# A gated graph layer on one core: the sums of the second layer start at -h, and the end stage takes their difference to h as it stands

## The chip, the cores and the metric

One Trainium2 chip, of which the kernel uses one core. The metric is the device time of one execution in microseconds, the median of several runs. The engines are named PE (TensorE, matrix products), DVE (VectorE), ACT (ScalarE), POOL (GpSimd) and SP (SyncE, which here only issues DMAs).

## What is computed

6250 nodes with 128 features, 200,000 edges sorted by their destination. Two graph layers follow one another. The change concerns the end of the second one. Cut to what matters (all in float32):

```
x1   = layernorm(x + layer0(x, edges))                 # first layer
h    = relu(layernorm(x1 @ W1 + b1) * g1 + bt1)
w    = sigmoid(relu([h[src], h[dst]] @ We1 + be1) @ We2 + be2)     # one weight per edge
aggr = segment_sum(w * h[src], dst)
gate = sigmoid([h, aggr] @ Wg + bg)                    # Wg: 256 x 128, its halves Wg_h and Wg_a
new  = gate * aggr + (1 - gate) * h
out  = layernorm(x1 + layernorm(new) * g2 + bt2)
```

## The kernel before

The nodes are 49 blocks of 128, taken in 13 groups of 4 (the last group has 1). Tensors named "cols" have features in the partitions and nodes in the columns: `sums[:, 0, :]`, called `aggr`, holds the sums of either layer that way, and `h_cols` holds h. Five stages follow one another:

1. Edges of layer 0 (to 402 us): sums of the edge features by destination, in `aggr`.
2. Middle stage (402 to 557 us), 13 groups through a pipeline over all engines: `mean_mm` (PE) reads a group of `aggr`; from it come x1, then h, then two tables in device memory, `src_table` and `dst_table`. The groups are interleaved by `run_stages` (L1969): at step t each engine does, in the order of its list, function f for group t - d, where d is the number beside f. On DVE the list is norm1 (4), pre (1), soft_sum (2), moments1 (3), norm2 (6), moments2 (5), rest (11), part2 (12), blank (3). On POOL it is residual (2) and gain (6); gain is two operations, L871 and L873. On ACT, h_turned (8) writes `h_cols` of a group. DVE's blank (L1763) sets the group's columns of `aggr` to zero, once mean_mm has read them, so that the sums of layer 1 can be added there.
3. Edge loop of layer 1 (557 to 2104 us): POOL gathers rows of `src_table` with one indirect DMA per 128 edges (L894), and DVE adds each result to its columns of `aggr` (L546).
4. End stage (from 2105.7 us), 13 groups: PE makes the gate's argument from `h_cols` and `aggr` (gate_mm, L1433 and L1434, two products of 512 columns each, of two PE instructions each), ACT the sigmoid (gate, L1175, into `pre`), POOL the difference aggr - h (apart, L914, into `soft`) and its product with the gate (mix_mul, L921, into `y1`), DVE adds h (mix, L1937, into `aggr`), PE transposes (mix_turn, L1287), ACT copies to `x_rows` (mix_out, L1180), and DVE takes mean and variance (moments3: L1722, L1725). `pre`, `soft` and `y1` have two buffers each, so mix_mul of group g waits for mix of group g - 2, and gate of group g for mix_mul of group g - 2. On DVE the order is mix (g), moments3 (g - 2); on PE gate_mm (g), mix_turn (g - 3); on POOL apart (g), mix_mul (g - 1).
5. Output stage (from 2149.7 us): normalization, g2, bt2, addition of x1, second normalization (L1734, four blocks a group), output. POOL has two operations a group there (L930, L934).

Waits: `need(eng, "name", g)` lets an engine wait until the step "name" has been done for group g. An engine takes its instructions in order.

The functions that the diff touches:

Of the kernel before, what the change touches and what calls it, by code (L numbers as in the profile page):

```python
# [17 lines left out]
ALU = mybir.AluOpType  # L18
# [5 lines left out]
P = 128  # L24
# [17 lines left out]
def gnn_pair(nc, n_nodes, n_edges, io):  # L42
# [13 lines left out]
    n_classes = len(CLASSES)  # L56
    tokens = SORTED * J
    class_cells = [n_blocks * cap for _, _, cap in CLASSES]
    class_cell0 = [sum(class_cells[:k]) for k in range(n_classes)]
    cells = sum(class_cells)  # L60
# [12 lines left out]
    for k, (_, _, cap) in enumerate(CLASSES):  # L73
        per = COLS // cap
        for b in range(0, n_blocks, per):
            riders_of.append((k, range(b, min(b + per, n_blocks))))
    n_riders = len(riders_of)
    GB = 4
    n_groups = -(-n_blocks // GB)
    blocks_of = [min(GB, n_blocks - GB * g) for g in range(n_groups)]  # L80
# [8 lines left out]
    with ctx:  # L89
        def sb(name, shape, dt=F32):  # L90
            return ctx.enter_context(nc.sbuf_tensor(name, shape, dt))

        def sem(name):
            return ctx.enter_context(nc.semaphore(name))
# [8 lines left out]
        aggr = sums[:, 0, :]  # L103
# [4 lines left out]
        h_cols = sb("h_cols", [P, padded])  # L108
# [56 lines left out]
        wg_h = sb("wg_h", [P, P])  # L165
        wg_a = sb("wg_a", [P, P])
# [37 lines left out]
        def temp(cols, dt=F32, depth=2):  # L204
            a = ring[:, at[0]:at[0] + cols * depth]
            at[0] += cols * depth
            a = a if dt == F32 else a.bitcast(dt)
            return a.rearrange("p (s c) -> p s c", s=depth)

        GC = GB * P  # L210
        pre = temp(GC)
        soft = temp(GC)
        y1 = temp(GC)
# [103 lines left out]
        place_dst = yard(2 * RIDE).rearrange("p (s k n) -> p s k n", s=2, k=COLS)  # L317
        cell_logit = yard(4 * COLS).rearrange("p (s k) -> p s k", s=4)
        U_SLOTS, BLOCKS = 3, COLS // min(cap for _, _, cap in CLASSES)
        src_part = spare_ring(U_SLOTS * BLOCKS * P).rearrange("p (s b f) -> p s b f", s=U_SLOTS, b=BLOCKS)  # L320
        h_part = spare_ring(U_SLOTS * BLOCKS * P).rearrange("p (s b f) -> p s b f", s=U_SLOTS, b=BLOCKS)
# [98 lines left out]
        def done(name):  # L420
            if name not in names:
                names[name] = sem("s_" + name)
            return names[name]

        def need(eng, name, n):

            if n >= 0:
                eng.wait_ge(done(name), n + 1)

        def loaded(eng, name, n=1):  # L430

            eng.wait_ge(done(name), 16 * n)
# [12 lines left out]
        def block_cols(g):  # L445
            return slice(g * GC, g * GC + blocks_of[g] * P)
# [339 lines left out]
        def _(eng):  # L786
# [80 lines left out]
            def gain(g):  # L867
# [4 lines left out]
                need(eng, "gain", g)  # L872
                eng.tensor_tensor(z, z, wide["bt1"][:, :].unsqueeze(1).to_broadcast([P, nb, P]), ALU.add).then_inc(done("offset"), 1)  # L873

            loaded(eng, "small", N_SMALL)
            loaded(eng, "x_rows", 2 if tail_nodes else 1)
            run_stages(n_groups, [(2, residual), (NORM2_AT, gain)])


            eng.wait_ge(done("mean_mm"), n_groups)  # L880
# [27 lines left out]

            eng.wait_ge(done("acc2_all"), 1)

            def apart(g):
                cols = block_cols(g)
                need(eng, "mix_mul", g - 2)
                eng.tensor_tensor(soft[:, g % 2, 0:blocks_of[g] * P], aggr[:, cols], h_cols[:, cols], ALU.subtract).then_inc(done("apart"), 1)  # L914

            def mix_mul(g):
                n = blocks_of[g] * P
                need(eng, "apart", g)
                need(eng, "gate", g)
                need(eng, "mix", g - 2)  # L920
                eng.tensor_tensor(y1[:, g % 2, 0:n], soft[:, g % 2, 0:n], pre[:, g % 2, 0:n], ALU.mult).then_inc(done("mix_mul"), 1)  # L921

            run_stages(n_groups, [(1, mix_mul), (0, apart)])


            for g in range(n_groups):
# [518 lines left out]
        def _(eng):  # L1445
# [16 lines left out]
            for g in range(row_groups):  # L1462
                n = min(P, n_chunks - g * P)
# [5 lines left out]
            for g in range(row_groups):  # L1469
                n = min(P, n_chunks - g * P)  # L1470
# [289 lines left out]
                need(eng, "part2", g - 2)  # L1760
                eng.tensor_tensor(r, bank[5][:, 0:nb * P].rearrange("p (b f) -> p b f", b=nb), three[:, :, 0, :], ALU.subtract).then_inc(done("rest"), 1)

            def blank(g):  # L1763
                need(eng, "mean_mm", g)
                eng.memset(aggr[:, block_cols(g)], 0.0)

            def part2(g):
                nb = blocks_of[g]
                three = dst_out[:, g % 2, 0:nb * PARTS * P].rearrange("p (b s f) -> p b s f", s=PARTS, f=P)
                r = rest[:, g % 2, 0:nb * P].rearrange("p (b f) -> p b f", b=nb)  # L1770
                need(eng, "part1", g)
                eng.tensor_tensor(three[:, :, 2, :], r, three[:, :, 1, :], ALU.subtract).then_inc(done("part2"), 1)

            run_stages(n_groups, [
                (4, norm1), (1, pre_), (2, soft_sum), (3, moments1_), (NORM2_AT, norm2), (5, moments2_),
                (DST_AT + 1, rest_), (DST_AT + 2, part2), (3, blank)])
            eng.drain()
            if columns > padded:
                step(eng.memset(aggr[:, padded:columns], 0.0))

# [183 lines left out]
NORM2_AT = 6  # L1964
DST_AT = 10
# [3 lines left out]
def run_stages(n, stages):  # L1969

    for t in range(n + max(d for d, _ in stages)):
        for d, f in stages:
            if 0 <= t - d < n:
                f(t - d)
# [34 lines left out]
```

## Time and profile before

| | us |
|---|---|
| median of 3 runs | 2201.44 |
| lowest and highest | 2198.95 and 2205.48 |
| the profiled execution | 2202.91 |
| its span | 2201.2 |
| middle stage | 402 to 557 |
| edge loop | 557 to 2104 |
| end stage up to the last mean and variance | 2105.7 to 2148.7 |
| output stage | 2149.7 to 2201.2 |

The span is what the profiler saw from the first instruction to the last; the execution's own time has 1.7 us more. Times of single instructions are given from the start of the span. In a timeline one row is one instruction, or several in a row of the same line and shape (x4), with their time together; a bracket behind it is the idle time of the engine before it and what ended that. The time of an instruction is from its issue to its end and includes what it waits for inside.

### The profile page before, as it was taken

To read this page: it belongs to the slowest core of one execution; us is meant where nothing else is said; L and a number is where in the kernel's file an instruction comes from. 1 tells how busy PE (TensorE), PEld (TensorE's weight loads), DVE (VectorE), ACT (ScalarE), POOL (GpSimd) and SP (SyncE) were. 2 spreads that over 40 slices of the span, in tenths; PEclk is the share of its full clock that TensorE was granted. 3 is DMA by queue.
4 is the path that set the end of the run, shared out by engine and by line. 5 is a ranking of instruction groups with operands and counts; after the bars stand their busy time and mean duration, and the time that the engine had idled before them with its cause. 6 is when DMAs were issued, how large, how long until landed. Compare 5 with 4: busy or idle time off the path is not lost.

```text
span 2201.2 us, 43991 instructions
## 1 busy us (share of the span) xinstructions
PE 1621.5 (74%) x13238; PEld 1452.1 (66%) x13239; DVE 1705.9 (77%) x7202; ACT 1070.7 (49%) x2826; POOL 1437.0 (65%) x1437
## 2 busy tenths in 40 slices
PE   4999996898477467777877877767667767877780
PEld 3777775776366467777777876766666667777640
DVE  7777886595899578887888887888876776777666
ACT  0111111375776046665666665766654544555325
POOL 4354430152777777777777777777777777777765
PEclk9999998687555557766767677898788786767675
DMA  7788898014544546556556566666666566666402
GB/s 275 261 298 286 289 336 286 27 47 157 176 127 138 159 127 177 169 170 181 172 166 181 158 181 189 179 189 181 176 198 195 173 193 192 188 188 186 131 1 59
DMA packets 279081, 394.16 MB, mean 179 GB/s; under 512 B 75155, under 2 KB 178612, under 8 KB 278715
## 3 DMA queue, kind: packets, MB, share of 16 engines
q1 hardware_dynamic: 217155, 226.47, 32.4%
q0 software_dynamic: 57408, 156.84, 24.5%
q10 hardware_dynamic: 4280, 8.03, 1.1%
q8 instruction: 107, 1.75, 0.3%
q14 instruction: 131, 1.07, 0.1%
HBM read 376.07 MB, written 15.12 MB: 178 GB/s over the span
## 4 chain that ended last, share of the span: by engine, by line
POOL 46%; PE 24%; issue 19%; DVE 7%; DMA 2%; DVEq 1%; ACTq 1%; ACT 1%; SPq 0%; POOLq 0%
POOL x_rows L894 34%; POOL ring L894 11%; PE bank L495 9%; PE bank L502 3%; PE bank L1289 3%; PE bank L542 2%; DVE bank L531 1%; PE bank L1261 1%; DMA x_rows<-src_table,lane_src 1%; DVE sums L1813 1%; PE bank L1233 1%; DMA ring<-src_table,lane_src 1%; DVE stats L1722 1%; PE bank L1298 1%; ACTq L974 1%
## 5 line engine op out<-in xcount | busy, mean ns | idle before, releaser
L894 POOL DMA_INDIRECT x_rows<-src_table,lane_src x900 | 888.9, 988 | 298.9 <-issue 271.8
L531 DVE SCALAR_TENSOR_TENSOR bank<-bank,we_all 128x128 f32<-128x128 f32 x1686 | 431.6, 324 | 11.1
L894 POOL DMA_INDIRECT ring<-src_table,lane_src x296 | 286.0, 966 | 90.2 <-issue 89.3
L546 DVE TENSOR_TENSOR sums<-sums,bank 128x128 f32 (+1 forms) x814 | 206.2, 253 | 150.1 <-issue 89.3
L1369 PE MATMUL bank<-ring,sums 128*128 128x128 f32 x980 | 274.1, 369 | 46.6 <-DVE bank L531 46.1
L527 DVE TENSOR_TENSOR bank<-bank,x_rows 128x512 f32<-128x512 f32 x225 | 146.4, 696 | 194.5 <-DMA x_rows<-src_table,lane_src 194.4
L1100 ACT ACTIVATE ring<-sums,be_all 128x4 f32<-128x4 f32 (+1 forms) x124 | 36.9, 297 | 508.8 <-DVE bank L531 508.8
L542 PEld LDWEIGHTS bank<-weighted,x_rows 128*128 128x128 f32 x1800 | 280.2, 245 | 0.0
L542 PE MATMUL bank<-weighted,x_rows 128*128 128x40 f32 x1800 | 279.0, 325 | 0.0
L522 PE MATMUL bank<-ring,onehot_t 120*128 120x128 bf16 x1196 | 135.7, 282 | 161.8 <-issue 84.6
L495 PE MATMUL bank<-ring 128*64 128x128 f32 x3128 | 221.8, 285 | 30.4 <-issue 25.3
L531 DVE DVE_READ_ACCUMULATOR bank<-bank,we_all 128x1 f32 x1686 | 235.7, 140 | 0.1
L1347 PE MATMUL bank<-sums 128*128 128x98 bf16 (+1 forms) x736 | 93.5, 299 | 187.9 <-issue 131.7
L1369 PEld LDWEIGHTS bank<-ring,sums 128*128 128x128 f32 x980 | 191.3, 242 | 53.1 <-DVE bank L531 53.0
L522 PEld LDWEIGHTS bank<-ring,onehot_t 120*128 120x128 bf16 x1196 | 109.9, 131 | 169.1 <-issue 168.3
L495 PEld LDWEIGHTS bank<-ring 128*64 128x64 f32 x3128 | 174.2, 140 | 55.0 <-issue 37.7
L1347 PEld LDWEIGHTS bank<-sums 128*128 128x128 bf16 x736 | 74.0, 131 | 203.2 <-issue 199.4
L995 ACT ACTIVATE ring<-bank 128x128 f32<-128x128 f32 x196 | 54.2, 277 | 298.7 <-PE bank L502 282.8
L1371 PE MATMUL bank<-ring,sums 128*128 128x128 bf16 x1470 | 197.3, 254 | 0.0
L1392 PE MATMUL bank<-sums 128*128 128x128 f32 x980 | 188.2, 356 | 0.0
L1392 PEld LDWEIGHTS bank<-sums 128*128 128x128 f32 x980 | 180.5, 275 | 0.0
L1134 ACT ACTIVATE sums<-sums,ones 128x512 f32<-128x512 f32 (+1 forms) x248 | 164.1, 709 | 8.8 <-issue 0.3
(250 smaller groups left out, 3386.2 us busy)
## 6 DMA issues: line engine op xcount, KB each, us to landing
ring<-in_edge_attr SPq DMA_DIRECT2D x195, 512.0 KB, 5.0
ring<-rel_table SPq DMA_DIRECT2D x74, 512.0 KB
ring<-cell_table SPq DMA_DIRECT2D x121, 256.0 KB
ring<-src_table SPq DMA_DIRECT2D x144, 128.0 KB
x_rows<-src_table,lane_src POOLq DMA_INDIRECT x900
ring<-dst_table SPq DMA_DIRECT2D x299, 32.0 KB
ring<-src_table SPq DMA_DIRECT2D x104, 64.0 KB
src_table<-ring SPq DMA_DIRECT2D x12, 512.0 KB, 3.7
```

The source lines that it names most:

```text
L495: last = eng.matmul(out, hot[:, j, :], v[:, j, :], start=(j == 0), stop=(j == J - 1), skip_group_check=True)
L522: last = eng.matmul(out[:, j, :], hot_t[:, j, :], win, start=True, stop=True, skip_group_check=True)
L527: return eng.tensor_tensor(out, out, rows_[:, :, 0:P], ALU.add)
L531: last = eng.scalar_tensor_tensor(hid[:, j, :], hid[:, j, :], 0.0, wide["we2"][:, :], ALU.max, ALU.mult, accum_out=out[:, j:j + 1])
L542: last = eng.matmul(out, rows_[:, j, P:2 * P], hot[:, j, :], start=(j == 0), stop=(j == J - 1))
L546: return eng.tensor_tensor(table[..., bass.ds(start, width)], table[..., bass.ds(start, width)], part, ALU.add)
L894: eng.indirect_dma_start(gathered(c)[:, j, :], None, src_table, bass.IndirectOffsetOnAxis(ap=lane_src[:, t:t + 1], axis=0)).then_inc(gathe ...
L1134: last = eng.activation(hot_, hot_, ACT.Relu, bias=ones[:, 0:1], scale=-1.0)
L1347: eng.matmul(cell_sums(k, v), rows_[:, i, v, :], cols_[:, i, :], start=(t == first and v == 0), stop=(t == end - 1), skip_group_check=True)
L1369: eng.matmul(o, src_hot[:, u % 2, e], src_part[:, u % U_SLOTS, col_block(u, i), :], start=True, stop=False, skip_group_check=True)
L1371: last = eng.matmul(o, dst_hot[:, u % 2, e], base_dst[:, k % 2, s, :], start=False, stop=(s == PARTS - 1), skip_group_check=True)
L1392: eng.matmul(weight_out(q, col_block(u, i)), place_src[:, u % 2, i, :], place_dst[:, u % 2, i, :], start=(i % cap == 0), stop=(i % cap == ...
```

## The change

POOL writes -h into a group's columns of `aggr` in the middle stage, in a new function less_h, in place of DVE's blank, which goes. The sums of layer 1 are then added to -h, so that `aggr` holds (sum - h) at the end. The end stage has no apart; mix_mul reads `aggr` directly. As the argument of the gate is now made from h and (sum - h), the weights of h become Wg_h + Wg_a, which POOL adds once. less_h waits for mean_mm and h_turned of its group and has the offset 9 in POOL's list. DVE waits for all of less_h in place of a drain before it clears the last columns of `aggr`.

```diff
@@ POOL, middle stage
+            def less_h(g):
+                need(eng, "mean_mm", g)
+                need(eng, "h_cols", g)
+                eng.tensor_scalar(aggr[:, block_cols(g)], h_cols[:, block_cols(g)], -1.0, None, ALU.mult).then_inc(done("less_h"), 1)
+
             loaded(eng, "small", N_SMALL)
             loaded(eng, "x_rows", 2 if tail_nodes else 1)
-            run_stages(n_groups, [(2, residual), (NORM2_AT, gain)])
+            eng.tensor_tensor(wg_h[:, :], wg_h[:, :], wg_a[:, :], ALU.add)
+            run_stages(n_groups, [(2, residual), (NORM2_AT, gain), (NORM2_AT + 3, less_h)])
@@ POOL, end stage
-            def apart(g):
-                cols = block_cols(g)
-                need(eng, "mix_mul", g - 2)
-                eng.tensor_tensor(soft[:, g % 2, 0:blocks_of[g] * P], aggr[:, cols], h_cols[:, cols], ALU.subtract).then_inc(done("apart"), 1)
-
             def mix_mul(g):
                 n = blocks_of[g] * P
-                need(eng, "apart", g)
                 need(eng, "gate", g)
                 need(eng, "mix", g - 2)
-                eng.tensor_tensor(y1[:, g % 2, 0:n], soft[:, g % 2, 0:n], pre[:, g % 2, 0:n], ALU.mult).then_inc(done("mix_mul"), 1)
-
-            run_stages(n_groups, [(1, mix_mul), (0, apart)])
+                eng.tensor_tensor(y1[:, g % 2, 0:n], aggr[:, block_cols(g)], pre[:, g % 2, 0:n], ALU.mult).then_inc(done("mix_mul"), 1)
+
+            for g in range(n_groups):
+                mix_mul(g)
@@ DVE, middle stage
-            def blank(g):
-                need(eng, "mean_mm", g)
-                eng.memset(aggr[:, block_cols(g)], 0.0)
-
@@
-                (DST_AT + 1, rest_), (DST_AT + 2, part2), (3, blank)])
-            eng.drain()
+                (DST_AT + 1, rest_), (DST_AT + 2, part2)])
+            eng.wait_ge(done("less_h"), n_groups)
             if columns > padded:
                 step(eng.memset(aggr[:, padded:columns], 0.0))
```

## Rows read from the trace of the kernel before

**Rows 1.** The page: busy time, share of the span and instructions of each engine

```profile
PE 1621.5 (74%) x13238; PEld 1452.1 (66%) x13239; DVE 1705.9 (77%) x7202; ACT 1070.7 (49%) x2826; POOL 1437.0 (65%) x1437
```

**Rows 2.** Timeline of POOL, end stage: start, duration, engine, line, operation

```profile
2123.15 1.27 POOL L914 TENSOR_TENSOR ring<-sums,h_cols 128x512 f32<-128x512 f32 x1
2124.50 1.60 POOL L921 TENSOR_TENSOR ring<-ring 128x512 f32<-128x512 f32 x1
...
2143.45 0.45 POOL L914 TENSOR_TENSOR ring<-sums,h_cols 128x128 f32<-128x128 f32 x1
```

**Rows 3.** Timeline of DVE, end stage

```profile
2121.99 0.86 DVE L1722 BATCH_NORM_STATS2 stats<-x_rows 128x6 f32<-128x128 f32 x4
2122.92 0.38 DVE L1725 BATCH_NORM_AGGREGATE ring<-stats 128x2 f32<-128x6 f32 x4
2123.23 1.74 DVE L1937 TENSOR_TENSOR sums<-ring,h_cols 128x512 f32<-128x512 f32 x1
...
2143.52 0.93 DVE L1937 TENSOR_TENSOR sums<-ring,h_cols 128x512 f32<-128x512 f32 x1
...
2148.56 0.18 DVE L1725 BATCH_NORM_AGGREGATE ring<-stats 128x2 f32<-128x6 f32 x1
```

**Rows 4.** Timeline of PE, end stage: the first two transposes

```profile
2115.32 0.60 PE L1287 MATMUL bank<-ident,sums 128*128 128x128 f32 x4
...
2117.48 0.60 PE L1287 MATMUL bank<-ident,sums 128*128 128x128 f32 x4
```

**Rows 5.** Timeline of ACT, end stage: the gate

```profile
2117.68 0.69 ACT L1175 ACTIVATE ring<-bank,bg_col 128x512 f32<-128x512 f32 x1 [0.98 <-PE bank L1434]
```

**Rows 6.** Windows: length, busy PE, PEld, DVE, ACT, POOL, granted clock, DMA

```profile
2105.70:2111.50 5.80, 5.80 (x8) 2.46 (x9) 0.00 (x0) 0.69 (x1) 2.44 (x2) 0.53 0.01 1
...
2123.20:2134.80 11.60, 9.49 (x34) 4.27 (x33) 11.31 (x38) 4.69 (x8) 11.29 (x9) 1.00 0.00 0
```

**Rows 7.** By line: duration ns min/median/max, first and last start, shape

```profile
L1765 DVE MEMSET sums<- x13: 165/485/485, 420.7 to 511.8; 128x512 f32 x12, 128x128 f32 x1
L819 POOL TENSOR_SCALAR x_rows<-x_rows x25: 1137/1152/1576, 43.6 to 282.4; 128x372 bf16<-128x372 f32 x25
```

**Rows 8.** Timeline of POOL, one step of the middle stage

```profile
448.07 1.26 POOL L871 TENSOR_TENSOR ring<-ring,g_all 128x512 f32<-128x512 f32 x1 [1.22 <-DVE ring L1734]
449.41 1.27 POOL L873 TENSOR_TENSOR ring<-ring,bt_all 128x512 f32<-128x512 f32 x1
453.15 1.27 POOL L865 TENSOR_TENSOR ring<-ring,x_rows 128x512 f32<-128x512 f32 x1 [2.46 <-DVE ring L1712]
```

**Rows 9.** Timeline of DVE, the same step, the two L1734 apart

```profile
448.86 0.38 DVE L1725 BATCH_NORM_AGGREGATE moments<-stats 128x2 f32<-128x6 f32 x4
449.30 0.48 DVE L1765 MEMSET sums<- 128x512 f32 x1
449.72 1.05 DVE L1734 TENSOR_SCALAR x_rows<-ring,moments,rstd 128x128 f32<-128x128 f32 x1
450.69 0.34 DVE L1734 TENSOR_SCALAR x_rows<-ring,moments,rstd 128x128 f32<-128x128 f32 x1
```

**Rows 10.** Timeline of DVE, output stage: the last of four L1734

```profile
2185.31 1.30 DVE L1734 TENSOR_SCALAR ring<-ring,moments,rstd 128x128 f32<-128x128 f32 x1
```

**Rows 11.** Timeline of POOL, output stage, the same time

```profile
2185.27 1.26 POOL L930 TENSOR_TENSOR ring<-ring,g_all 128x512 f32<-128x512 f32 x1 [0.47 <-ACT ring L1196]
```

**Rows 12.** Timeline of DVE, middle stage from 480 us

```profile
480.88 0.59 DVE L1734 TENSOR_SCALAR x_rows<-ring,moments,rstd 128x128 f32<-128x128 f32 x2
...
487.75 1.50 DVE L1772 TENSOR_TENSOR ring<-ring 128x512 bf16<-128x512 f32 x1
```

**Rows 13.** Waits, 442 to 512 us: who waited for whom, total, times, longest

```profile
DVE stats L1722 <- PE bank L1291: 2.5, 3, 1.5
```

**Rows 14.** The chain that ended last, end of the middle stage: start, us, what

```profile
550.12 4.65 DMA dst_table<-ring
```

**Rows 15.** Timeline of ACT, middle stage: the last group of h_cols

```profile
535.17 0.28 ACT L1062 ACTIVATE h_cols<-bank 128x128 f32<-128x128 f32 x1 [0.42 <-PE bank L1287]
```

## The prediction, made before the changed kernel ran

> **What bounds the kernel now.** I read first the page's busy line [rows 1]: no engine is full over the span, so the share of an engine prices nothing here, and only the two stretches that the change touches matter. These are the stage over 13 node groups before the gathers (402 to 557 us) and the end stage (2105.7 us on). Between them lies the edge loop, which the change does not touch.
>
> I took the end stage next, engine by engine in order of time. On POOL [rows 2] each full group has one L914 subtraction of 1.27 us and one L921 product of 1.60 us, without idle time; from the start of one L914 (2123.15) to the end of the L921 behind it (2126.1), where the next L914 begins, is 2.9 us. DVE [rows 3] in the same group has four statistics (0.86), four aggregates (0.38) and the L1937 addition (1.74). It looks full too, but the 1.74 us is mostly waiting: the last full addition, behind the short L914 of 0.45 us, took 0.93 us. The addition starts 0.08 us after L914, and whichever started first keeps the other out. With L914 done at 2124.42, 0.55 us are left for the addition's own work (to 2124.97); and L921, started 0.47 us before that, is lengthened from 1.26 to 1.60. So a period is 1.27 + 0.55 + 1.13 less small overlaps: two POOL operations and one DVE operation one behind the other. PE [rows 4] shows its own pace where nothing yet holds it: from the transposes of one group (2115.32) to those of the next (2117.48) 2.155 us. ACT needs 0.69 us a group for the gate [rows 5]. The granted clock is 1.00 (2.4 GHz) in the middle of the stage [rows 6], and PE is busy 9.49 of 11.60 us there. The order of limits is POOL with DVE 2.90, then PE 2.155, then DVE alone 0.86 + 0.38 + 0.55 = 1.8, then ACT and POOL alone, about 1.3.
>
> The Trainium skill says in SBUF — State Buffer, section "SBUF: two separate sides", that VectorE and GpSimd share a port pair as an exclusive lock held for a whole instruction, and that a VectorE operation with two SBUF inputs needs it against a GpSimd operation that reads SBUF. By this rule the added subtraction-by-sign in the middle stage is not free beside DVE even where POOL is idle. What it does here is worked out from rows below and is the first rival.
>
> **End stage, step by step.** Removed: 13 L914, so POOL has 1.26 us a group and PE becomes the bound. Nothing changes before the first gates (PE sets them, and its slow clock at first, 0.53 of full by rows 6's first line, stays). From the first transposes at 2115.32 the PE sequence goes on at 2.155 us: the transposes of group 8, which stand behind the last full gate matmuls, start at 2115.32 + 8 x 2.155 = 2132.56. Then 0.1 to wake ACT, gate 0.69, 0.1, product 1.26: 2134.7. The short last product (0.45, as L914 of that size) may come first; then the addition 0.55 and 0.1: 2135.8. From the end of that addition to the last aggregate are, before, 2144.45 to 2148.74, that is 4.29 us [rows 3], all DVE work that stays. So the stage ends at 2140.1 in place of 2148.74: **8.6 us gained**. Were the additions always caught behind the next product, a group would cost 1.26 + 0.55 + two handovers of 0.08 = 1.97, still under PE's 2.155. The bounds: 7.5 (two groups held up as now) and 9.2 (no delay from the last short product). The output stage behind it has the same work. The one addition of the weights on POOL is 128 x 128 (0.45 us) and runs while POOL waits, before the first group: nothing.
>
> **Middle stage: what is removed.** 13 DVE memsets, 0.485 us each [rows 7]. The step at 449 us [rows 8, 9] shows why they bought little: the aggregates end at 449.24, the memset follows, then the first normalization of L1734 is issued at 449.72 and stays blocked until L873 ends at 450.68 (1.05 us for an operation that takes 0.33 unblocked), and the second ends at 451.02. The memset sits in the shadow of L871 and L873. Without it the first normalization can slip in between L871 and L873 (issued at 449.2, L871 ends 449.33, L873 starts 449.41), but the second still waits for L873, and is then done 0.25 us sooner. Gain 0 to 0.25 us a step in 5 steps: I take 0.5 us in all, as PE is full in part of them.
>
> **What is added.** 13 tensor_scalar on POOL. No row shows one of this form. L819, 372 columns, takes 1.15 us [rows 7], so 512 columns by its rate are 1.6 us; the low end is 0.45, the 128-column tensor_tensor. I take 1.6, by the nearest operation of the same kind. The Trainium skill, GPSIMD Engine Reference, section 4.1, calls one-input elementwise work on GpSimd roughly line-rate, and its section 3.1 gives 769 ns for 512 elements in the best case; L819 here is slower than that. By the page the middle stage would lose about 0.3 us in place of the 2.0 that I take below.
>
> POOL has the time (it waits 2.46 us in each step for L1712 before its residual, L865 [rows 8], and the new operation falls into that wait), and h_cols, which it waits for, is two ACT steps old. What is queued behind it is the next residual (L865), not late. What counts is DVE. less_h stands directly behind L873, and a second DVE operation then loses to it. The output stage shows how such a race goes [rows 10, 11]: a POOL operation started at 2185.27, the fourth normalization of a run of four was issued at 2185.31, and it took 1.30 us in place of 0.33. The cases by step:
> - groups 0 and 1 of less_h (steps 10 and 11, at 465 and 473): the first normalization has slipped in before L873, the second is already waiting when L873 ends, and goes before less_h. Nothing lost.
> - group 2 (480.9): the L1761 operation stands before the normalizations, so the first takes the gap behind L873 and the second waits for less_h. Both were done at 481.47 [rows 12], now about 482.6: 1.1 us.
> - groups 3 to 6 (488 to 512): part2 (L1772) is held by L873, 1.50 us [rows 12], of which 0.55 are its own; less_h, waiting since L873's end, goes next, and the normalizations wait about 1.1 to 1.5 us for it. DVE has some time in hand for that: three waits for PE's products, 2.5 us together [rows 13], and the memset's 0.4 us a step. What is left is about 0.35 us a step, 1.4 in all.
> - groups 7 to 12: DVE is idle for most of the time from 512 on; nothing.
> Sum: -0.5 + 1.1 + 1.4 = **2.0 us lost** (bounds: 1 gained, 0.25 in each of 4 steps, if the slack hides the rest; 7.7 lost if the second normalization loses in steps 10 and 11 too and no slack hides any of the seven, 7 x 1.1).
>
> **What lies behind it.** The first gathers wait for the last source rows, and the edge loop starts behind the last DMA of the destination table, at 550.12 + 4.65 [rows 14]. Both are at the end of the same chain, so the loss moves them. The new wait in front of DVE's last memset, for all of less_h, is over by about 537 (h_cols of the last group is written at 535.17 [rows 15]), and DVE comes to it only when that DMA's wait is over, 18 us later. POOL's two iotas move behind less_h, and DVE needs them after the same point. So both are hidden.
>
> **Sum.** -8.6 + 2.0 = -6.6 us. The profiled execution took 2202.91 (span 2201.2 and 1.7 around it), so 2196.3 for it; it stood 1.5 above the median, 2201.44, so the median comes to **2194.8**.
>
> **Rivals.**
> 1. The port eats the gain: each less_h from step 9 to 16 holds DVE up by its whole length, 8 x 1.6 = 12.8 lost against 8.6 gained, 2201.4 + 4.2 = 2205.6, slower than before. For it: both engines' blocked operations above; against: DVE idles in steps 13 to 16, and the blocked one must be the second of two. It decides from 1.1 us a step on. Chance 0.08.
> 2. The middle stage hides less_h, or it is short: 0 to 1 gained there, 8.6 in the end stage: 2192.3 (2201.4 - 9.1). For it: idle DVE time behind 490 us; a length of 0.45 to 0.8. Against: L819. Chance 0.24.
> 3. The end stage does not hold PE's pace. PE at the half clock needs 2.155 us more for a group (its first groups before 2111, granted 0.53). Three such groups cost 6.5: 2201.3. Against: the granted clock was 1.00 with PE less busy than it will be. Chance 0.10.
> 4. The edge loop, started at another moment, runs otherwise against its DMAs, by half of what the runs of before differ (3.3 us) either way: 2191.5 or 2198.1. Nothing in the loop is touched. Chance 0.06.
> The forecast itself (2192.5 to 2197.5) has 0.52.
>
> **Numbers.** This kernel's runs lie 6.5 us apart, 0.3%; a change of less than that (2194.8 to 2208.0 stays inside) cannot be told from none. The forecast lies on that edge: half of its 0.52, all of rival 2 and a third of 4 are faster by over 0.3%, in all 0.52; slower by over 0.3% needs rival 1 with more than 15 us lost, 0.03; the rest, 0.45, is within. Range 2190.5 to 2201.
>
> **What would show it.** In the end stage: additions (L1937's successor) near 0.6 us in place of 1.74, transposes 2.15 us apart, the last aggregate about 34.4 us behind the first gate matmul in place of 43.0. In the middle: less_h near 1.6 us; steps until 480 us up to 0.25 us shorter; a second normalization blocked from 480 on; the first L894 gather about 2 us later, near 551. I am wrong if the period stays above 2.5 us, if less_h is under 1 us, or if the first gather moves by more than 6 us.

## The result, and the profile after

The changed kernel took 2192.36 us (median of 5 runs, 2190.23 to 2192.95), the kernel before beside it 2202.09 (5 runs, 2198.95 to 2205.48): ratio 0.9952, 95% interval 0.9937 to 0.9966, that is 9.7 us. Two later timings of the same kernel gave 0.9958 (0.9944 to 0.9972) and 0.9960 (0.9945 to 0.9975), so about 9 us. The profiled execution took 2192.95, its span 2191.2. New lines: less_h L879, the product L922, gathers L901, moments L1724 and L1727, the normalization L1736, part2 L1770, DVE's addition L1935, transposes L1289.

| Stretch, us | before | after | difference |
|---|---|---|---|
| span's start to the first gather | 548.93 | 548.80 | -0.13 |
| from there to the cast behind the edge loop | 1554.97 | 1554.36 | -0.61 |
| cast to the first gate matmul | 1.77 | 1.77 | 0 |
| first gate matmul to the end of the last aggregate | 43.07 | 34.98 | -8.09 |
| from there to the span's end | 52.47 | 51.26 | -1.21 |

The page's busy line, answering to [rows 1]: POOL lost the 13 subtractions and won 13 less_h and the one addition of the weights, and DVE lost its 13 memsets.

```profile
PE 1621.5 (74%) x13238; PEld 1453.0 (66%) x13239; DVE 1691.1 (77%) x7189; ACT 1069.9 (49%) x2826; POOL 1437.2 (66%) x1438
```

POOL in the end stage after, against [rows 2]; the brackets give the idle time before a row and who ended it:

```profile
2122.26 1.31 POOL L922 TENSOR_TENSOR ring<-sums,ring 128x512 f32<-128x512 f32 x1 [0.84 <-ACT ring L1177]
2124.42 1.32 POOL L922 TENSOR_TENSOR ring<-sums,ring 128x512 f32<-128x512 f32 x1 [0.84 <-ACT ring L1177]
...
2133.04 1.73 POOL L922 TENSOR_TENSOR ring<-sums,ring 128x512 f32<-128x512 f32 x2 [0.85 <-ACT ring L1177]
```

DVE in the same group, and its last aggregate, against [rows 3]:

```profile
2122.70 0.87 DVE L1724 BATCH_NORM_STATS2 stats<-x_rows 128x6 f32<-128x128 f32 x4 [0.26 <-ACT x_rows L1182]
2123.65 0.38 DVE L1727 BATCH_NORM_AGGREGATE ring<-stats 128x2 f32<-128x6 f32 x4
2123.95 0.66 DVE L1935 TENSOR_TENSOR sums<-ring,h_cols 128x512 f32<-128x512 f32 x1
...
2139.72 0.18 DVE L1727 BATCH_NORM_AGGREGATE ring<-stats 128x2 f32<-128x6 f32 x1
```

PE's transposes, against [rows 4]: those of groups 0, 1 and 8.

```profile
2114.83 0.60 PE L1289 MATMUL bank<-ident,sums 128*128 128x128 f32 x4
...
2116.99 0.60 PE L1289 MATMUL bank<-ident,sums 128*128 128x128 f32 x4
...
2132.08 0.60 PE L1289 MATMUL bank<-ident,sums 128*128 128x128 f32 x4
```

The same window as the second of [rows 6]:

```profile
2123.20:2134.80 11.60, 10.98 (x49) 6.26 (x47) 9.89 (x52) 7.15 (x13) 7.36 (x7) 1.00 0.00 1
```

POOL now waits 0.84 us a group for the gate, and DVE 0.26 for the rows; PE waits for neither. The period is 2.155 us from the first transposes on (17.25 us for eight groups), and the addition, which now comes where POOL idles, takes 0.66 in place of 1.74. The granted clock stayed at 1.00 (2.4 GHz).

### The profile page after: what moved, and what is told of

Read it like the earlier page. It is cut to its first block, busy times and chain, and to the rows that moved or that the text cites. A ratio compares the mean times of both kernels' runs of the same rounds, so it can differ in the third digit from the quotient of the medians.

```text
span 2191.2 us, 43990 instructions
## 1 busy us (share of the span) xinstructions
PE 1621.5 (74%) x13238; PEld 1453.0 (66%) x13239; DVE 1691.1 (77%) x7189; ACT 1069.9 (49%) x2826; POOL 1437.2 (66%) x1438
## 4 chain that ended last, share of the span: by engine, by line
POOL 38%; PE 30%; issue 17%; DVE 9%; DMA 4%; DVEq 1%; ACTq 1%; ACT 1%; SPq 0%; POOLq 0%
POOL x_rows L901 29%; PE bank L495 9%; POOL ring L901 9%; PE bank L542 3%; PE bank L502 3%; PE bank L1291 2%; DVE bank L531 2%; DMA x_rows<-src_table,lane_src 2%; PE bank L1371 1%; PE bank L1394 1%; PE bank L1263 1%; PE bank L1402 1%; PE bank L522 1%; PE bank L1373 1%; DVE sums L1811 1%
## 5 line engine op out<-in xcount | busy, mean ns | idle before, releaser
L901 POOL DMA_INDIRECT x_rows<-src_table,lane_src x900 | 889.7, 989 | 287.5 <-issue 269.9
L901 POOL DMA_INDIRECT ring<-src_table,lane_src x296 | 285.2, 963 | 90.2 <-issue 88.6
L542 PEld LDWEIGHTS bank<-weighted,x_rows 128*128 128x128 f32 x1800 | 284.9, 248 | 0.3 <-issue 0.3
L495 PE MATMUL bank<-ring 128*64 128x128 f32 x3128 | 221.4, 284 | 31.2 <-issue 26.2
```

The lines of the kernel that those rows point to most:

```text
L495: last = eng.matmul(out, hot[:, j, :], v[:, j, :], start=(j == 0), stop=(j == J - 1), skip_group_check=True)
L542: last = eng.matmul(out, rows_[:, j, P:2 * P], hot[:, j, :], start=(j == 0), stop=(j == J - 1))
L901: eng.indirect_dma_start(gathered(c)[:, j, :], None, src_table, bass.IndirectOffsetOnAxis(ap=lane_src[:, t:t + 1], axis=0)).then_inc(gathe ...
```

## The experiments

All timings of one group share a chip and the runs of the kernel before: 23 runs, median 2207.5 (2197.75 to 2211.44), for the end stage alone, the middle stage alone, the changed kernel again and the first timing of early h.

**The end stage alone.** The memsets stay and less_h is out; the subtraction goes, and the product reads the sums, which start at zero, so the gate multiplies the sums without the minus h.

```
-    def apart(g): ... subtract ...
-    need(eng, "apart", g)
-    tensor_tensor(y1[...], soft[...], pre[...], mult)
+    tensor_tensor(y1[...], aggr[:, block_cols(g)], pre[...], mult)
```

> The end stage of the changed kernel (no apart, mix_mul reads aggr) on the middle stage of before. Left out: the subtraction of h from the sums. If the gain is all in the end stage, as forecast: end stage 35.0 us from the first gate matmul to the last aggregate in place of 43.1, time 8.1 us under before, ratio 0.9963. Rival (part of the gain is in the middle stage): 5 us or less under before.

Measured: 2197.43 us, 12 runs, ratio 0.9959 (0.9943 to 0.9976), 9 us. In the traces the stretch from the cast to the last aggregate's start is 35.6 us; with the old end stage six traces of three kernels gave 44.7 to 44.9, with the new one the changed kernel gave 36.6, 36.2 and 35.6. What differs among these three is how early PE's granted clock rises from 0.5 in the first gate matmuls: the first transposes come 11.68, 11.28 and 10.75 us behind the cast, and from there to the last aggregate's start all three take 24.9. With the old end stage the same spread (11.11 to 11.78 us) leaves the stretch as it is. So the 8.09 us of the first pair of traces is the low end: this one gives 9.1, and the timing 9. The end stage alone carries a gain as large as that of the whole change.

**The middle stage alone.** Memsets out, less_h in, weights summed; the end stage keeps its subtraction, which then takes h off a second time. The cut shows DVE's part against the kernel before.

```
-    (DST_AT + 1, rest_), (DST_AT + 2, part2), (3, blank)])
-    eng.drain()
+    (DST_AT + 1, rest_), (DST_AT + 2, part2)])
+    eng.wait_ge(done("less_h"), n_groups)
```

> The middle stage of the changed kernel with the end stage of before (apart stays, and subtracts h a second time). By the forecast 2 us slower than before; by the trace of the changed kernel 0 to 1.5 us faster; end stage 43.1 us as before. Rival (the middle stage was worth several us): 3 us or more faster than before.

Measured: 2204.66, 11 runs, ratio 0.9987 (0.9978 to 0.9996). The prediction had it 2 us slower; here it is 1 to 5 us faster, but this first timing did not repeat (below).

**The changed kernel again**, for the same chip.

> The changed kernel once more, with its own profile. If the middle stage's net effect is an effect of the added and removed operations, the first gather starts within 0.5 us of the first profile (146 us behind the start of the stage) and the steps have the same lengths. If it is set by when PE's clock is granted, the steps differ by some us from profile to profile. End stage 35.0 us and output stage 51.3 us again if both are fixed; 52.5 us for the output stage if it drifts by chance.

Measured: 2198.05, 6 runs, ratio 0.9958. That is 9.3 us, where the two parts alone gave 9.0 and 2.9: the change is worth its end stage, and what the middle stage adds is within these intervals' width.

**What the middle stage takes without a change.** One execution each of the kernel before and of it without its memsets (the sums then start from what the memory holds); beside them a trace of early h, which is the changed kernel with an edit in the end stage only (below).

> The kernel before, with another profile. If the 1.2 us by which the output stage is shorter in the changed kernel is chance, its output stage here is 51.3 us too in place of 52.5. If it comes with the change, 52.5 again. The middle stage shows how far its steps lie apart between two profiles of one program: under 0.5 us if fixed, some us if the granted clock moves them.

> The kernel before without DVE's memsets of the middle stage, and nothing in their place; left out is the clearing of the sums. By the forecast's term the steps from 442 to 480 us are up to 0.25 us shorter each and the first gather starts 0.5 us earlier. If less_h costs what the forecast said, the first gather is here 1 to 3 us earlier than in the changed kernel; if less_h is hidden, within 0.5 us of it.

Measured: 2206.28 and 2206.24 us, one execution each, beside 2208.85 for one of the kernel before; single executions that lie so close decide nothing, so the traces are read. The first gather is 4.6 us later in the second trace of the kernel before than in its first, so the middle stage is not fixed to 0.5 us; its output stage is 52.5 us again.

Windows of the three, cut at POOL's residuals of groups 0, 4, 9 and 12 and at the first gather; the columns are those of [rows 6]. First the kernel before, second execution:

```profile
413.90:435.37 21.47, 19.18 (x89) 16.66 (x88) 16.15 (x73) 13.00 (x29) 5.08 (x4) 0.58 0.00 0
435.37:474.44 39.07, 37.63 (x199) 32.35 (x198) 36.00 (x156) 26.00 (x60) 19.02 (x16) 0.69 0.08 28
474.44:502.40 27.96, 26.10 (x148) 20.69 (x147) 20.68 (x90) 18.58 (x45) 11.40 (x9) 0.88 0.19 64
502.40:553.49 51.09, 45.76 (x217) 32.77 (x216) 22.83 (x77) 24.23 (x55) 11.84 (x13) 0.75 0.48 155
```

Without the memsets:

```profile
414.39:435.49 21.10, 19.02 (x89) 16.68 (x88) 14.73 (x70) 12.74 (x28) 5.07 (x4) 0.58 0.00 0
435.49:474.19 38.70, 37.46 (x199) 32.22 (x198) 35.47 (x151) 25.55 (x60) 19.38 (x16) 0.69 0.08 28
474.19:501.93 27.74, 25.88 (x147) 20.21 (x146) 19.41 (x87) 18.68 (x45) 11.39 (x9) 0.88 0.18 59
501.93:552.70 50.77, 44.29 (x220) 31.80 (x219) 22.39 (x75) 24.12 (x55) 11.83 (x13) 0.79 0.49 159
```

Without the memsets and with less_h (the kernel called early h below):

```profile
415.29:436.48 21.19, 19.00 (x88) 16.65 (x88) 14.72 (x70) 12.71 (x28) 5.08 (x4) 0.58 0.00 0
436.48:475.40 38.92, 37.70 (x199) 32.30 (x198) 35.41 (x151) 25.64 (x60) 22.18 (x18) 0.69 0.09 28
475.40:503.14 27.74, 25.88 (x147) 20.20 (x146) 19.40 (x87) 18.68 (x45) 15.77 (x12) 0.88 0.18 59
503.14:553.90 50.76, 44.29 (x220) 31.80 (x219) 23.01 (x75) 24.11 (x55) 22.61 (x22) 0.79 0.49 159
```

In the first three windows all three were granted 0.58, 0.69 and 0.88, so these can be compared: they sum to 88.50, 87.54 and 87.85 us. The memsets cost 0.96 and less_h 0.3. To the first gather the sums are 139.59, 138.31 and 138.61, that is 1.28 and 0.30, but in the last window the first kernel was granted 0.75 and the others 0.79. A fourth trace, the second of the changed middle stage alone, was granted the same as early h and has less_h too: 87.78 us in three windows, 138.91 to the first gather, so less_h costs 0.2 to 0.3 in the three windows and 0.3 to 0.6 to the first gather. In the window with groups 2 to 4 it costs nothing (27.74 in both).

A mean grant over a window is not enough for such a comparison. Without the memsets a second execution took 39.39 us for the second window, at 0.69 as before and 0.69 us longer, with the grants spread otherwise over its steps; in the four traces used here they agree step by step to about 0.03. Where the grants differ, so do the lengths: the kernel before took 134.47 for the same work in its first trace, granted 0.50, 0.86 and 0.93, and the changed kernel 136.04, 132.75 and 141.13 in its three. A comparison of two traces of this stage with different grants can be off by more than 5 us, more than either edit.

**The two edits of the middle stage, timed.** This group shares 29 runs of the kernel before, median 2204.63 (2197.12 to 2210.8).

> The kernel before without its 13 memsets; its sums then start from what the memory holds, so the output leaves out that the sums start at zero. Theory (the middle stage depends on the memsets by 0.2 us a step in five steps, as two traces with the same granted clock in each part showed: 139.59 against 138.31 us from the first residual to the first gather): 1.3 us faster than before, 0.5 to 2.5. Rival (the prediction's term): 0.5. Second rival (the memsets cost their whole busy time beside a full VectorE): 13 x 0.485 = 6.3 us faster.

> The middle stage of the change alone (memsets out, less_h in, weights summed), the end stage as before; the end stage's subtraction then takes h off twice. Theory (less_h holds VectorE only for its first 0.6 us and mostly where VectorE does not want the port): within 0.8 us of no_blank_again, 0.3 slower by the traces, so some 1 us faster than before. Rival, the prediction's two terms (1.1 and 1.4 us): 2.5 us slower than no_blank_again and 2 slower than before.

Measured: without memsets 2206.53, 12 runs, ratio 1.0010 (0.9996 to 1.0025); with less_h as well 2205.63, 12 runs, ratio 1.0005 (0.9992 to 1.0017). The expected gain of 1.3 us for the first is not there (its interval goes from 0.9 us faster to 5.5 slower), and the rival of 6.3 faster is out. less_h against none: 0.9 us faster by the medians, 0.5 by the means, where the prediction's terms have 2.5 slower; the means' difference is uncertain by more than 1 us, so the timing leans against 2.5 and does not measure 0.3. The two timings of the changed middle stage barely agree (0.9987 and 1.0005). Weighted by their intervals they give 1.5 us faster, 0 to 3, and 1.2 of that is the output stage's, which is shorter in both (below). By this estimate the middle stage itself comes out at nothing, within 1.6 us, and the 2.0 us slower of the prediction lies just outside.

**Why less_h costs so little.** less_h was changed to a subtraction with two inputs, h minus h, so that the sums start at zero and the minus h is left out.

```
-    tensor_scalar(aggr[...], h_cols[...], -1.0, None, mult)
+    tensor_tensor(aggr[...], h_cols[...], h_cols[...], subtract)
```

> less_h as a two-input operation of the same size (h minus h, so the sums start at zero; left out is the -h). It takes 1.26 us in place of 1.49. In the changed kernel a DVE operation with two SBUF inputs was held only when it was issued in the first 0.6 us of less_h. If that is because less_h reads one input and is done with reading early, the same DVE operations are held here for the whole 1.26 us (L1770 issued inside it takes up to 1.5 us), and the first gather starts 0.5 to 3 us later. If the operand count does not matter, the holds are as before and the stage is as long or shorter.

Measured: 2201.25 us in one execution, against 2208.85 for the kernel before beside it. The changed kernel, POOL, the less_h of groups 4 and 5:

```profile
494.31 1.49 POOL L879 TENSOR_SCALAR sums<-h_cols 128x512 f32<-128x512 f32 x1
...
502.72 1.49 POOL L879 TENSOR_SCALAR sums<-h_cols 128x512 f32<-128x512 f32 x1
```

DVE in the changed kernel: part2 in these two groups and, last, one with no less_h about, for its free duration.

```profile
495.47 0.69 DVE L1770 TENSOR_TENSOR ring<-ring 128x512 bf16<-128x512 f32 x1
...
502.95 0.92 DVE L1770 TENSOR_TENSOR ring<-ring 128x512 bf16<-128x512 f32 x1
...
529.29 0.68 DVE L1770 TENSOR_TENSOR ring<-ring 128x512 bf16<-128x512 f32 x1
```

With the two-input form, POOL:

```profile
500.19 1.04 POOL L879 TENSOR_TENSOR sums<-h_cols 128x512 f32<-128x512 f32 x1
```

and DVE, in the same group:

```profile
500.39 1.38 DVE L1770 TENSOR_TENSOR ring<-ring 128x512 bf16<-128x512 f32 x1
```

The one-input form lets part2 run inside it: at 495.47, 0.33 us before less_h ends, it takes 0.69, nothing more than free. Issued 0.23 us after less_h's start it is held 0.24, so it works from 0.47 us after the start; another (522.49, 1.09 long, less_h at 522.43) gives 0.47 again. The two-input form, shorter by itself, holds it from 500.39 for 0.70 us, to 0.90 of its 1.04; a second case (less_h at 529.28, part2 at 529.36 for 1.50) gives 0.90 again. So the form of the POOL operation sets how long it holds DVE. Whether it is the number of inputs or the kind of instruction was not separated. The whole stage took 140.95 us here, but under other grants, so what that costs the kernel was not separated.

The hold goes both ways. In the changed kernel's second execution part2 came 0.02 us first, and less_h was the one that lost (2.13 in place of 1.49). DVE:

```profile
485.82 0.68 DVE L1770 TENSOR_TENSOR ring<-ring 128x512 bf16<-128x512 f32 x1
```

POOL:

```profile
485.84 2.13 POOL L879 TENSOR_SCALAR sums<-h_cols 128x512 f32<-128x512 f32 x1
```

**What bounds the end stage next.** The gate without its product of h (that part of the gate is left out), so PE has less to do.

```
-    matmul(bank[...], wg_h, h_cols[...], start=True, stop=False)
-    matmul(bank[...], wg_a, aggr[...], start=False, stop=True)
+    matmul(bank[...], wg_a, aggr[...], start=True, stop=True)
```

> The changed kernel without the gate's product of h (left out of the result), so that PE has 0.86 + 0.44 = 1.3 us a group. The forecast gives 1.97 us a group as the pace of POOL with DVE: the end stage is then 13 x 0.2 = 2 us shorter, plus the cold first products, some 4 us in all. If POOL alone is the bound (no hold), 1.35 us a group and 10 us less.

Measured: 2187.12 in one execution; cast to last aggregate 33.0 us, 2.6 to 3.6 less than in the changed kernel. POOL:

```profile
2118.20 1.27 POOL L922 TENSOR_TENSOR ring<-sums,ring 128x512 f32<-128x512 f32 x1 [0.69 <-DVE sums L1934]
2120.16 1.27 POOL L922 TENSOR_TENSOR ring<-sums,ring 128x512 f32<-128x512 f32 x1 [0.69 <-DVE sums L1934]
```

DVE:

```profile
2119.20 0.81 DVE L1934 TENSOR_TENSOR sums<-ring,h_cols 128x512 f32<-128x512 f32 x1
```

The period is 1.96 us: product 1.27 and 0.69 until DVE's addition, held since 2119.20, is done. That is the floor of 1.97 that the prediction worked out from before. With PE taken off the path, POOL and DVE take over at once, so more speed on PE is worth 0.2 us a group.

**Early h.** The first gate matmuls run at half clock behind a wait of 2.55 us for the last sums, though half of them need only h. Here PE issues those of groups 0 and 1 ahead of the wait:

```
+    for g in range(min(2, n_groups)):
+        gate_h(g)
     eng.wait_ge(done("acc2_all"), 1)
     ...
-        matmul(bank[...], wg_h, h_cols[...], start=True, stop=False)
+        if g >= 2:
+            gate_h(g)
```

> The changed kernel, with the gate's product of h for groups 0 and 1 issued by PE ahead of the wait for the last sums. If PE sets the end stage from its first product on, its idle 2.5 us there are filled: the end stage is 2.5 us shorter counted from DVE's last addition, time 2.5 us under the changed kernel (about 2190). If POOL with DVE is the bound by now, nothing: within 0.5 us.

Measured: 2194.88, 5 runs, ratio 0.9938 (0.9924 to 0.9953). Timed once more, beside the changed kernel:

> The changed kernel. Sum of the parts as the traces showed them: end stage 8.1 to 8.5 us and middle stage 1.0 to 1.3, so 9.3 to 9.8 us faster than before (ratio 0.9956). If the output stage's 1.1 us is a part of it: 10.6 (0.9952). By the prediction's terms: 6.6 (0.9970).

> The changed kernel with the gate's products of h for groups 0 and 1 issued before the wait for the last sums. Theory (TensorE sets the end stage, but VectorE's additions there fall under the next product and keep half of the start's gain): 1.6 us faster than after_third, by the stretch from the last cast to the last aggregate (34.8 us against 36.2 and 36.6). Rival 1 (the whole shorter start, 3.1 us, counts): 3.1 faster. Rival 2 (the difference of the last timing was chance): within 0.5 us of after_third.

Measured: the changed kernel 2195.65 (12 runs), ratio 0.9960 (0.9945 to 0.9975); early h 2189.41 (6 runs), ratio 0.9946 (0.9925 to 0.9966). Early h is the faster in both groups, by 3.2 and 6.2 us of the medians (2.5 and 5.5 of the means, 4.4 and 3.1 by the ratios); it beats both kernels. The ratios' intervals overlap, and how much more than the expected 1.6 us it is stays open. In the second timing's trace the edge loop, which the edit does not touch, happened to take 1549.2 us, 5 to 7 less than in the changed kernel's traces. In the traces the stretch from the cast to the last aggregate is 34.8 and 34.1 us, against 36.6, 36.2 and 35.6: about 1.7 less. In the first trace the first transposes come 8.62 us behind the cast in place of 11.68, so 3.1 were gained there, and over 40% of it was given back by the last aggregate. POOL in early h:

```profile
2125.09 1.27 POOL L922 TENSOR_TENSOR ring<-sums,ring 128x512 f32<-128x512 f32 x1 [0.88 <-ACT ring L1177]
```

DVE in early h:

```profile
2125.60 0.38 DVE L1734 BATCH_NORM_AGGREGATE ring<-stats 128x2 f32<-128x6 f32 x4
2125.90 1.00 DVE L1942 TENSOR_TENSOR sums<-ring,h_cols 128x512 f32<-128x512 f32 x1
2126.82 0.86 DVE L1731 BATCH_NORM_STATS2 stats<-x_rows 128x6 f32<-128x128 f32 x4
```

The addition is issued at 2125.90, inside a product that runs to 2126.36, and takes 1.00; DVE has no idle time and comes out one product late in every group, to the last. In the changed kernel it is issued behind the product (2123.95 and 2126.10, products ending at 2123.57 and 2125.74). Both phases repeat themselves at the same period of 2.155 us.

## Why the prediction came out as it did

The mechanism of the end stage was right, and the time, 2194.8, was 2.4 us too high. Against the spans, which differ by 10.0 us where 6.6 were forecast, the end stage gave 0.5 less than its term, the middle stage lost nothing that the runs can show where 2.0 were to be lost, the output stage gave 1.2 that no term had, and the edge loop 0.6. By its steps:

- **End stage, -8.6:** measured -8.09 here. The pace of PE, 2.155 us, and the stage's 17.24 us over eight groups came out (17.25). Of the 34.4 us forecast, 34.98 came: 0.26 more before the first transposes (9.91 us behind the first gate matmul in place of 9.65) and 0.3 more behind those of group 8, where the last full addition ends at 3.30 us (forecast 3.24) and the work from there to the last aggregate takes 4.52 in place of 4.29. The 0.26 is the time by which PE's granted clock rose later than in the first trace of the kernel before. The 4.52 has one statistics instruction, at 2139.34, that comes 0.2 us late with nothing in the trace to wait for (more on such below). The port rival's basis, that a product and an addition exclude each other, is real (0.66 against 1.00 and 1.74); PE's pace left room for both.
- **Middle stage, +2.0: this step failed, by size.** The first gather was to come 2 us later, near 551, and came at 548.80. That alone decides nothing: the stage began 1.7 us earlier (first residual at 412.75 in place of 414.47) and took 1.57 longer, with other grants (0.64, 0.73 and 0.87 against 0.50, 0.86 and 0.93). What decides is the traces with equal grants and the timings. The first term, the memsets, was -0.5; the traces showed -1.0 where the grants are equal, the timing none. The normalizations behaved as forecast: in the changed kernel the first comes at 452.99, before L873 at 453.13, and the three steps between 449 and 471 us took 7.37 in place of 7.56. Its other terms, 1.1 and 1.4 us for holds by less_h, were to be 2.5; the traces with equal grants showed 0.2 to 0.6. The duration was nearly right (1.49 against 1.6, by the rate of L819). What failed is the premise that less_h holds DVE for all of it: part2 runs inside a less_h or waits for its first 0.47 us. In group 2 the two normalizations lost 0.4 us, not 1.1.
- **Port:** in the changed kernel a one-input POOL operation lets a two-input DVE operation run before its end. The rule cited from the Trainium skill (SBUF — State Buffer, "SBUF: two separate sides") has the lock held for the whole instruction; here that is nearly so for two-input operations (0.90 of 1.04 us) and not for the one-input one (0.47 of 1.49).
- **Length:** less_h took 1.49 us for 512 columns. The Trainium skill's GPSIMD Engine Reference, section 3.1, gives 769 ns for 512 elements in the best case; less_h took nearly twice that. The 0.3 us lost that the prediction works out from the page is nearer to what came than its own 2.0, but for another reason: less_h is as long as was taken, and holds DVE for less of it.
- **Rival 2** (the middle stage hides less_h, 2192.3) is the case that happened; its condition was taken to be idle time or a short less_h, and neither was it. That its number was met within 0.1 us is luck: it has 8.6 in the end stage, where 8.1 came, and nothing in the output stage, where 1.2 came. Rivals 1 and 3 did not occur: the kernel is not slower, and the granted clock in the middle of the end stage stayed at 1.00. Rival 4 is met below.
- **The output stage, taken as unchanged, gave 1.2 us**, and this is a side effect of the change that the prediction did not see. Counted from the last aggregate's start to the span's end it is 52.6 us in three traces (the kernel before twice, the end stage alone) and 51.4 to 51.5 in the eleven others. The three have the same program on DVE (the end stage alone differs on POOL only); the eleven have one without the memsets. Up to 28.2 us behind the last aggregate's start all is alike. Then one aggregate comes 0.2 to 0.3 us late with nothing in the trace to wait for: in the three at 31.2 us, in the eleven at 34.5. DVE in the second trace of the kernel before:

```profile
2182.63 0.31 DVE L1725 BATCH_NORM_AGGREGATE moments<-stats 128x2 f32<-128x6 f32 x3
...
2183.08 0.18 DVE L1725 BATCH_NORM_AGGREGATE moments<-stats 128x2 f32<-128x6 f32 x1
...
2186.97 2.93 DVE L1734 TENSOR_SCALAR ring<-ring,moments,rstd 128x128 f32<-128x128 f32 x4 [0.64 <-ACT rstd L1030]
```

The changed kernel, DVE, with the late aggregates and the same four normalizations:

```profile
2173.80 0.25 DVE L1727 BATCH_NORM_AGGREGATE moments<-stats 128x2 f32<-128x6 f32 x2
2174.22 0.25 DVE L1727 BATCH_NORM_AGGREGATE moments<-stats 128x2 f32<-128x6 f32 x2 [0.17 <-issue]
2175.11 1.43 DVE L1736 TENSOR_SCALAR ring<-ring,moments,rstd 128x128 f32<-128x128 f32 x4 [0.64 <-ACT rstd L1032]
```

and POOL:

```profile
2176.70 1.26 POOL L932 TENSOR_TENSOR ring<-ring,g_all 128x512 f32<-128x512 f32 x1 [1.00 <-ACT ring L1198]
```

The four normalizations take 2.93 us against 1.43, and the difference lies in the last of them. In the three traces it is issued 36.75 us behind the last aggregate's start, 0.04 to 0.05 behind POOL's operation, and is held for all of that: it is the very case of [rows 10, 11]. In the eleven it is issued at 36.5 and done at 36.8, and POOL's operation begins at 37.0 (here 2176.70; the normalizations end at 2176.54). What follows is 1.2 us later in the three. So the place of the late aggregate goes with DVE's program in all fourteen traces, and the hold that costs the 1.2 us stands in the rows; that the one brings about the other was not tested, nor what makes the aggregate late. The eleven have one more such instruction just before the last aggregate of the end stage (the 0.2 us above).
- **The edge loop** gave 0.6 here. It took 1549.2 to 1559.5 us in the traces, and 1553.7 to 1555.3 in those of the kernel before and of most others, with no order by kernel. Rival 4 gave this 3.3 us either way; single executions of the loop spread wider than that, but not by the change.

Open: whether the middle stage gives 1 us or costs 1 (its two timings differ by 4 us and hold the output stage's 1.2 us gain as well), and how much of early h's gain in the timing is more than its 1.7 us in the traces.

## What to carry to other kernels

Remove an operation from the engine that sets the period and work out the next limit at once, with the operations of its neighbours that exclude each other: here 2.9 fell to PE's 2.155, and the 1.96 below it was the true floor of the other two engines. Price work moved to an idle engine by the time in which it keeps another out, which differs from its duration, and by the place where it falls in the neighbour's order. Before two traces of one stage are compared, put the granted clocks of its parts side by side.

## What the runs showed of the hardware

- POOL's tensor_scalar of 128 x 512 f32 took 1.49 us, its tensor_tensor with both inputs from different tiles 1.26 and with twice the same input 1.04. The one-input form is the longest of them and holds DVE least.
- That hold is not one piece at the start alone: in group 2 of the changed kernel, with less_h at 476.47, the normalization at 477.03 was free (0.34) and the next, at 477.29, took 0.75. What the pieces are was not settled.
- The middle stage took 134.5 or 139.6 us in two executions of the kernel before, with grants of 0.50, 0.86, 0.93 and 0.58, 0.69, 0.88 in its first three parts, and 132.8 to 141.1 in three of the changed kernel. Its spread from one execution to another, with the granted clock, is nearly as large as what the whole change gave; the edge loop's, 1549.2 to 1559.5, is as large.
- Single instructions on DVE come 0.2 to 0.3 us late with nothing to wait for, at places that are fixed for a program: at 31.2 us of the output stage in three traces with one program, at 34.5 in eleven with another. The output stage of the three was longer by 1.2 us.
- A pair of engines that exclude each other can settle in either of two phases of the same period and keep it (addition 0.66 or 1.00 us, to the stage's end).
